# Stores of 16 KB rows from a separate output ring, drained in 32-partition quarters

## The reference

```
w = weights[subjects]                       # (128, 128, 128), one matrix for each sample
out = x + jnp.einsum('bct,bcd->bdt', x, w)  # f32, as large as x
```

## Time and profile before

| | |
|---|---|
| median of three runs | 325.02 us |
| profiled execution, its own time | 324.45 us |
| its span, first to last instruction | 322.8 us |
| granted TensorE clock, mean | 0.918 of 2.4 GHz |
| DMA moved | 134.80 MB, mean 418 GB/s |

### The profile page before, as it was taken

The page is one execution under the profiler, slowest core; times in us unless marked ns, Lnnn a source line. Parts: engine busy times, 40 slices in busy tenths (PEclk is TensorE's granted clock), DMA queues, the critical chain, the costliest instruction groups (busy, mean ns, idle before and its releaser), DMA issues.

```text
span 322.8 us, 3820 instructions
## 1 busy us (share of the span) xinstructions
PE 248.9 (77%) x1032; PEld 116.9 (36%) x1032; DVE 160.2 (50%) x130; ACT 133.9 (41%) x132; POOL 52.8 (16%) x137
## 2 busy tenths in 40 slices
PE   3499999999978866888868787669878687886400
PEld 1144444444434433334424343324334243443100
DVE  0426776776763636452645534353725555254600
ACT  1024664656552424444534434242724444243400
POOL 2031221222220101111211111010201111000000
PEclk9879999999997998997989999987979899799955
DMA  7999999999999999999999999999999999999994
GB/s 275 422 421 417 425 427 427 423 428 426 428 428 426 426 429 427 427 426 428 427 427 429 425 428 428 427 426 429 428 424 430 428 425 428 428 426 427 428 427 209
DMA packets 18455, 134.80 MB, mean 418 GB/s; under 512 B 1041, under 2 KB 2066, under 8 KB 2066
## 3 DMA queue, kind: packets, MB, share of 16 engines
q1 hardware_dynamic: 9744, 67.64, 50.0%
q10 hardware_dynamic: 8706, 67.11, 49.1%
HBM read 67.63 MB, written 67.11 MB: 417 GB/s over the span
## 4 chain that ended last, share of the span: by engine, by line
DMA 43%; PE 41%; issue 4%; DVE 3%; ACT 1%; DVEq 1%; POOLq 0%; ACTq 0%; POOL 0%; SPq 0%
PE products L143 39%; DMA out<-ring 27%; DMA ring<-x 15%; DVE ring L169 3%; PE products L125 2%; DMA loaded<-weights 1%; ACT ring L184 1%; DVEq L39 1%; DVE table L156 1%; POOLq L109 0%; POOL selected L114 0%; ACTq L192 0%; DVEq L163 0%; SPq L82 0%; ACTq L178 0%
## 5 line engine op out<-in xcount | busy, mean ns | idle before, releaser
L143 PE MATMUL products<-ring,selected 64*128 64x512 f32 x1024 | 242.7, 629 | 48.2 <-DVE ring L169 37.0
L169 DVE COPY ring<-products 64x1024 f32<-64x1024 f32 x128 | 156.4, 1222 | 135.1 <-PE products L143 133.1
L184 ACT COPY ring<-products 64x1024 f32<-64x1024 f32 x128 | 128.7, 1006 | 164.6 <-PE products L143 162.9
L143 PEld LDWEIGHTS products<-ring,selected 64*128 64x128 f32 x1024 | 114.5, 199 | 176.3 <-issue 128.1
L114 POOL COPY selected<-table 64x256 f32 x128 | 51.0, 398 | 232.1 <-PE products L143 185.4
L125 PE MATMUL products<-loaded,spread 128*128 128x512 f32 x8 | 6.2, 946 | 5.3 <-DMA loaded<-weights 5.3
L156 DVE TENSOR_TENSOR table<-products,unit 128x1024 f32<-128x1024 f32 x2 | 3.9, 1938 | 9.6 <-PE products L125 9.6
L184 ACT ACT_TABLE_LOAD x4 | 5.1, 1283 | 6.0 <-DVE ring L169 2.9
L125 PEld LDWEIGHTS products<-loaded,spread 128*128 128x128 f32 x8 | 2.4, 312 | 8.3 <-issue 8.3
L98 POOL TENSOR_SCALAR_AFFINE_SELECT unit<-ones 64x256 f32<-64x256 f32 x2 | 0.8, 404 | 0.1
L90 POOL TENSOR_SCALAR_AFFINE_SELECT spread<-ones 128x256 f32<-128x256 f32 x1 | 0.4, 418 | 0.1
## 6 DMA issues: line engine op xcount, KB each, us to landing
ring<-x SPq DMA_DIRECT2D x32, 2048.0 KB, 24.1
out<-ring ACTq DMA_DIRECT2D x32, 2048.0 KB, 42.1
loaded<-weights SPq DMA_DIRECT2D x1, 512.0 KB, 4.3
subject_row<-subjects ACTq DMA_DIRECT2D x1, 0.5 KB
```

The source lines that it names most:

```text
L143: last = nc.tensor.matmul(products[:, b, g, n * BANK:(n + 1) * BANK], selected[part, k, e * mixed:(e + 1) * mixed], ring[part, s, e * time ...
L169: nc.vector.tensor_copy(ring[0:HALF, s, b * times:(b + 1) * times], products[b * HALF:(b + 1) * HALF, s % PSUM_BUFS, 0, :]).then_inc(even_ ...
L184: nc.scalar.copy(ring[HALF:channels, s, b * times:(b + 1) * times], products[b * HALF:(b + 1) * HALF, s % PSUM_BUFS, 1, :]).then_inc(odd_d ...
```

## The change

The output no longer goes back into `ring`. `ring` shrinks to 8 tile slots (4 groups) and only holds x; a new `out_ring` has 4 slots of one group. An output row is now four channels of a sample (16384 B) on one of 32 partitions, so a group of four samples fills 128 partitions with one row each. The table's output columns are permuted to match. A sample's product leaves PSUM as four copies of 32 partitions x 1024 instead of two of 64: sixteen copies a group, nine on ACT (2, 3, 2, 2 for the four samples) and seven on DVE, where both engines read from the same sample. SP reloads a slot of x once PE has finished with it, instead of once its store has landed. ACT and DVE wait at the head of a group until the store of the group four back has landed. A turn is 8 tiles, so there are 8 turns.

```
-TILES_PER_TURN = 16
+TILES_PER_TURN = 8
+SIDE = 4
+QUARTER = 32
+ACT_COPIES = (2, 3, 2, 2)
+DVE_COPIES = tuple(SIDE - n for n in ACT_COPIES)
-DRAINED_FREE = 2 * PSUM_BUFS
+ACT_FREE = sum(ACT_COPIES)
+DVE_FREE = sum(DVE_COPIES)
-    out_rows = out.rearrange("b (q e) t -> (b q) (e t)", e=2).rearrange("(t p) f -> p t f", p=channels)
+    out_rows = out.rearrange("b (q e) t -> (b q) (e t)", e=SIDE).rearrange("(t p) f -> p t f", p=channels)
+        out_ring = ctx.enter_context(nc.sbuf_tensor("out_ring", [channels, groups, SIDE * times], F32))
...
# SP
+                sp.sem_inc(stored[s // SPAN], DMA)
...
-                    sp.wait_ge(stored[s // SPAN], turn * DMA + DMA)
+                    sp.wait_ge(product_ready, PRODUCT_FREE + tile + SPAN)
# PE
-                    pe.wait_ge(even_drained, DRAINED_FREE + 2 * (tile - PSUM_BUFS) + 2)
-                    pe.wait_ge(odd_drained, DRAINED_FREE + 2 * (tile - PSUM_BUFS) + 2)
+                    group = turn * groups + s // SPAN
+                    pe.wait_ge(dve_drained, DVE_FREE * group + sum(DVE_COPIES[:2 * (s % SPAN) + 2]))
+                    pe.wait_ge(act_drained, ACT_FREE * group + sum(ACT_COPIES[:2 * (s % SPAN) + 2]))
# ACT; DVE has the same with range(ACT_COPIES[i], SIDE)
+                    if s % SPAN == 0:
+                        act.wait_ge(stored[s // SPAN], turn * DMA + DMA)
                     act.wait_ge(product_ready, PRODUCT_FREE + tile + 1)
-                    for b in range(2):
-                        nc.scalar.copy(ring[HALF:channels, s, b * times:(b + 1) * times],
-                                       products[b * HALF:(b + 1) * HALF, s % PSUM_BUFS, 1, :]
-                                       ).then_inc(odd_drained, 1)
+                    for g in range(2):
+                        i = 2 * (s % SPAN) + g
+                        for b in range(ACT_COPIES[i]):
+                            nc.scalar.copy(out_ring[i * QUARTER:(i + 1) * QUARTER, s // SPAN,
+                                                    b * times:(b + 1) * times],
+                                           products[b * QUARTER:(b + 1) * QUARTER, s % PSUM_BUFS, g, :]
+                                           ).then_inc(act_drained, 1)
...
+                        act.wait_ge(act_drained, ACT_FREE * group + 2 * ACT_FREE)
+                        act.wait_ge(dve_drained, DVE_FREE * group + 2 * DVE_FREE)
+                        act.dma_start(out_rows[:, bass.ds(group, 1), :], out_ring[:, s // SPAN:s // SPAN + 1]
+                                      ).then_inc(stored[s // SPAN], DMA)
```

More of the change, by code:

```diff
@@ L29, in subject_mix_kernel @@
     banks = times // BANK
+    groups = TILES_PER_TURN // SPAN
     wide = 2 * mixed
@@ L65, in subject_mix_kernel @@
         product_ready = sem("product_ready")
-        even_drained = sem("even_drained")
-        odd_drained = sem("odd_drained")
+        dve_drained = sem("dve_drained")
+        act_drained = sem("act_drained")
         block = ctx.enter_context(nc.Block())
@@ L151, in _ @@
         def _(dve):
-            dve.sem_inc(even_drained, DRAINED_FREE)
+            dve.sem_inc(dve_drained, DVE_FREE)
             dve.wait_ge(unit_ready, 2)
@@ L156, in _ @@
                 nc.vector.tensor_tensor(
[L157 to L160, removed]
+                    table[:, :, e * mixed:(e + 1) * mixed].rearrange("p n (b m) -> p n m b", b=SIDE),
+                    products[:, 0, e, :].rearrange("p (n m b) -> p n m b", n=n_subjects, b=SIDE),
+                    unit[:, e * mixed:(e + 1) * mixed].rearrange("p (m b) -> p m b", b=SIDE).unsqueeze(1).to_broadcast(
+                        [channels, n_subjects, QUARTER, SIDE]),
                     ALU.add).then_inc(table_ready, 1)
@@ L165, in _ @@
                     tile = turn * TILES_PER_TURN + s
+                    if s % SPAN == 0:
+                        dve.wait_ge(stored[s // SPAN], turn * DMA + DMA)
                     dve.wait_ge(product_ready, PRODUCT_FREE + tile + 1)
-                    for b in range(2):
-                        nc.vector.tensor_copy(ring[0:HALF, s, b * times:(b + 1) * times],
-                                              products[b * HALF:(b + 1) * HALF, s % PSUM_BUFS, 0, :]
-                                              ).then_inc(even_drained, 1)
+                    for g in range(2):
+                        i = 2 * (s % SPAN) + g
+                        for b in range(ACT_COPIES[i], SIDE):
+                            nc.vector.tensor_copy(out_ring[i * QUARTER:(i + 1) * QUARTER, s // SPAN,
+                                                           b * times:(b + 1) * times],
+                                                  products[b * QUARTER:(b + 1) * QUARTER, s % PSUM_BUFS, g, :]
+                                                  ).then_inc(dve_drained, 1)
         @block.scalar
@@ L175, in _ @@
             act.dma_start(subject_row[:], subjects.rearrange("(a b) -> a b", a=1)).then_inc(subjects_loaded, DMA)
-            act.sem_inc(odd_drained, DRAINED_FREE)
+            act.sem_inc(act_drained, ACT_FREE)
             with act.Fori(0, turns) as turn:
@@ L180, in _ @@
                     tile = turn * TILES_PER_TURN + s
+                    if s % SPAN == 0:
+                        act.wait_ge(stored[s // SPAN], turn * DMA + DMA)
                     act.wait_ge(product_ready, PRODUCT_FREE + tile + 1)
-                    for b in range(2):
-                        nc.scalar.copy(ring[HALF:channels, s, b * times:(b + 1) * times],
-                                       products[b * HALF:(b + 1) * HALF, s % PSUM_BUFS, 1, :]
-                                       ).then_inc(odd_drained, 1)
-                    if s % SPAN == SPAN - 1:
[L189 to L193, removed]
+                    for g in range(2):
+                        i = 2 * (s % SPAN) + g
+                        for b in range(ACT_COPIES[i]):
+                            nc.scalar.copy(out_ring[i * QUARTER:(i + 1) * QUARTER, s // SPAN,
+                                                    b * times:(b + 1) * times],
+                                           products[b * QUARTER:(b + 1) * QUARTER, s % PSUM_BUFS, g, :]
+                                           ).then_inc(act_drained, 1)
+                    if s % SPAN == SPAN - 1:
+                        group = turn * groups + s // SPAN
+                        act.wait_ge(act_drained, ACT_FREE * group + 2 * ACT_FREE)
+                        act.wait_ge(dve_drained, DVE_FREE * group + 2 * DVE_FREE)
+                        act.dma_start(out_rows[:, bass.ds(group, 1), :], out_ring[:, s // SPAN:s // SPAN + 1]
+                                      ).then_inc(stored[s // SPAN], DMA)
             for s in range(0, TILES_PER_TURN, SPAN):
-                act.wait_ge(stored[s // SPAN], turns * DMA)
+                act.wait_ge(stored[s // SPAN], turns * DMA + DMA)
 def kernel(x, itok_B_0_7, L0_cond_weights):
```

## The result

The changed kernel takes 368.35 us (median of four runs, 366.35 to 369.19); the kernel before, on the same chip, 325.16 us. The ratio is 1.1313, 95% interval 1.1293 to 1.1334: slower by 13%. The forecast was 370 us. The profiled execution of the changed kernel took 368.83 us, its span is 367.1 us.

What follows compares the result with a forecast made beforehand. Before the change the DMA was taken as the bound, after it ACT: 22.11 + 240.7 + 81.2 + 9.50, then 8.0 + 0.8, PE's clock 6.0 and 1.65 around the span give 369.9, rounded to 370 us; range 352 to 386.

Steps and rivals of the forecast that it cites:

- 24 groups inside a turn: On ACT, each group not at a turn's head takes 9.28 + 0.22 + 0.38 + 0.15 = 10.03 us, 240.7 us in all.
- 7 heads: On ACT, seven groups at the start of a turn take 11.60 us each with a repeated table load, 81.2 us.
- last store to the span's end: After the last issue, the lone store takes 8.0 us to land and the span goes on for 0.8 us.
- Copies: PSUM drain: a 32-partition copy costs what a 64-partition one does, 1006 ns on ACT, 1222 on DVE; ACT's nine take 9.28 us.
- The rival in which copies shrink: PSUM drain: copies get shorter with fewer partitions and the DMA stays the bound, 323.8 to 328.2 us; chance 0.06.
- the one in which both engines take turns on a bank: PSUM reads: ACT and DVE alternate on one bank, 18.0 + 0.75 us a group, over 600 us; chance 0.02.
- The store on ACT: ACT's stream per group: 0.22 us to the issue, 0.38 us issuing, 0.15 us register steps for the next waits.
- The head: Start of a turn on ACT: table load repeated, 1.30 us, and 0.42 us of register steps; such a group takes 11.60 us.
- The rival with a drain behind each load: Turn heads on ACT: the pipeline empties at each table load, about as long again, 378.9 us; chance 0.02.
- PE's clock: PE after its rests: lowered clock makes tiles 0.69 us late for ACT in 0.36 of 24 groups, 6.0 us.
- Loads: Reloads of x: the first is issued at 25.5 us, the DMA idles about 3.7 us, costing nothing while ACT bounds.
- Rows of 16384 B: Stores: packets fall from 8192 to 4096, worth 0 to 4.4 us of DMA time, nothing on the path.

## Why the prediction was right

The forecast, ACT as the bound, is what the runs show, and 370 us stands 1.65 us above the median. Its terms against the profiled execution:

| term | predicted | measured |
|---|---|---|
| ACT's first copy | 22.11 us | 20.87 us |
| 24 groups inside a turn | 24 x 10.03 = 240.7 us | 24 x 9.91 = 237.8 us |
| late tiles of PE in them | 6.0 us | 11.3 us |
| 7 heads | 7 x 11.60 = 81.2 us | 81.0 us |
| last group to its store | 9.50 us | 9.45 us |
| last store to the span's end | 8.8 us | 6.75 us |
| span | 368.3 us | 367.1 us |

- *Copies*: right. The bound from above held to 3 ns (1003 against 1006 ns, 1225 against 1222), 9.28 us foreseen for nine and 9.22 measured. The rival in which copies shrink is out, and so is the one in which both engines take turns on a bank, since neither copy grew.
- *The store on ACT*: 0.75 us foreseen, 0.69 measured. Taken away, it gave 29 us: 24 x (9.91 - 9.23) + 7 x (11.57 - 10.53) = 23.6 us of its own, and 7.3 us of late tiles (11.3 before, 4.0 left), less 1.7 us of a later start (22.56 us against 20.87), which has nothing to do with the store: the same kernel with its stores cut in two started at 20.84.
- *The head*: 1.30 us for the load plus 0.42 - 0.15 us of loop; 11.57 against 11.60. The rival with a drain behind each load is out: the load ends at 62.93, the copy starts at 62.95, and the seven heads are alike. The drain that "ScalarE: Activation LUTs" of the Trainium skill adds for a switch to a different set (section "What ACT_TABLE_LOAD costs") did not show at these heads; whether any of these loads is such a switch, no run here shows.
- *PE's clock*: the mechanism was right, the term was mis-sized, 6.0 us against 11.3. I counted about nine late groups (24 x 0.36) at 0.69 us each; there were ten, five of them 0.70 us late as foreseen and five 0.5 to 2.0 us (7.7 us in all). These five stand right behind a head, where PE had rested 3.76 us, and in four of them nearly the whole first tile, not only a part of it, ran at half the clock. I had the head hide a late tile, which it did twice (at 56.52 and 227.18 us), and left out that PE rests longer there: the tile behind such a rest was late in five cases of five.
- *Loads*: the DMA does idle near 24 us (a share of 0.10 from 24 to 25 us), for about 2 us and not 3.7. Alone, with ACT out of the way, the split costs 4 us. The last store, alone, landed 6.3 us after its issue and not 8.0.
- *Rows of 16384 B*: 0 to 4.4 us of DMA time was too wide a bound; the kernel with stores on SP against its version with two halves shows 428 against 427 GB/s and no measurable time. "DMA: Bandwidth & Descriptors" of the Trainium skill, section "Why small descriptors are slow (HBM only)", has a fixed overhead of about three cycles a packet. An estimate from that figure: three cycles on the 256 beats of 32 B of an 8192 B row are 1.2%, and half as many packets save 0.6% of the stores' half of the DMA time, about 1 us. The runs do not speak against it, but cannot tell 1 us from nothing.
- What I had not foreseen at all is that the stores of longer rows overtake the loads when each has a queue of its own. In the changed kernel it costs nothing, since PE never waits for x there.

The errors cancel, and that is luck: -1.2 at the start, -2.9 inside turns, +5.3 for the clock, -2.1 at the end. The mechanism and the sizes of a group and a head were foreseen; a sum this close was not.

## What to carry to other kernels

A copy of 1024 f32 out of PSUM cost the same on 32 partitions as on 64 (1003 against 1006 ns on ACT, 1225 against 1222 on DVE), so halving the partitions of each copy doubled the drain. Before a change that adds instructions to an engine with idle time, add up that engine's whole stream in one period, its DMA issues, waits and loop heads included, and set it against the period that the bound leaves (here 9.91 to 11.57 us against 9.82). A DMA issue or a table load in the stream of the bounding engine also lengthens the rests of the engines behind it; count what they do after a longer rest.

## What the runs showed that was not expected

- With stores of 16384 B rows on ACT's queue and loads of 8192 B rows on SP's, stores landed in 12.0 us and loads in 29.6; in one queue 32.1 and 29.8. In the kernel before, with 8192 B rows on both queues, it was 42.1 and 24.1.
- Writing out ACT's loop shortened a group inside a turn from 9.91 to 9.68 us, not only the heads.
- A tile of PE behind a rest was slow (its burst took longer than at the full clock) in 5 of 5 cases at a rest of 3.76 us and in 7 of 14 at 2.1 us in the changed kernel, in 12 of 18 at 1.9 us without ACT's loop, in none of 10 and 12 at 1.8 us in the same two kernels, where the tile before had been slow, and in none of 50 at 1.4 us in the two kernels with stores on SP. So the length of the rest alone does not decide it.
